# The sum over states in a Mamba scan: identity matmuls in VectorE's layout in place of accumulated transposes, a copy and transposes back

## What is computed

```python
def step(h, e):                      # h: (batch, 512 channels, 16 states)
    da, dbu, c = e
    h = da * h + dbu                 # the scan over time
    y = jnp.einsum('bdn,bn->bd', h, c)   # the sum over states
    return (h, y)
_, ys = jax.lax.scan(step, h0, elems)
y = jnp.moveaxis(ys, 0, 1) + u * D
y = y * jax.nn.silu(z)
out = jnp.einsum('bld,ed->ble', y, W_out)
```

## Time and profile before

| what | value |
|---|---|
| median of 3 runs | 1965.84 us (1965.61 to 1968.22) |
| span of the profiled execution | 1972.5 us, 16625 instructions |
| PE busy | 1592.9 us (81%) |
| DVE busy | 1595.6 us (81%) |
| ACT busy | 1005.4 us (51%) |
| POOL busy | 842.5 us (43%) |
| mean granted TensorE clock | 0.869 |

### The profile page before, as it was taken

One profiled execution on the slowest core, in us unless ns is written; L12 is line 12 of the kernel. 1 busy time (PEld: TensorE's weight loads), 2 busy tenths in 40 slices (PEclk: granted clock), 3 DMA queues, 4 the chain that ended last, 5 costly groups with the idle time before them and its releaser, 6 DMA issues. The chain is left out here.

```text
span 1972.5 us, 16625 instructions
## 1 busy us (share of the span) xinstructions
PE 1592.9 (81%) x5776; PEld 842.8 (43%) x5776; DVE 1595.6 (81%) x1686; ACT 1005.4 (51%) x1609; POOL 842.5 (43%) x443
## 2 busy tenths in 40 slices
PE   6767877798888789887888779987888879976954
PEld 2445334443455245543455235453445334452423
DVE  4895879957997989978998889979899789973264
ACT  4542755356563656446563655636553655633511
POOL 0764365515553265515554265614555155520000
PEclk9767788787899789997899889997899879987977
DMA  4000000000000000000000000000000000000000
GB/s 151 1 0 11 12 0 0 11 13 0 1 0 18 6 11 1 11 12 0 11 0 11 12 11 0 0 23 0 11 0 11 12 0 11 0 11 11 1 11 11
DMA packets 18057, 20.51 MB, mean 10 GB/s; under 512 B 1360, under 2 KB 16976, under 8 KB 18016
## 3 DMA queue, kind: packets, MB, share of 16 engines
q1 hardware_dynamic: 18016, 19.98, 3.1%
HBM read 15.79 MB, written 4.19 MB: 10 GB/s over the span
## 5 line engine op out<-in xcount | busy, mean ns | idle before, releaser
L393 POOL TENSOR_TENSOR reg_a<-reg_a,cb 128x1024 f32<-128x1024 f32 x256 | 603.7, 2359 | 495.9 <-DVE reg_a L1099 495.9
L1099 DVE TENSOR_TENSOR_SCAN reg_a<-reg_a,pb 128x1024 f32<-128x1024 f32 x256 | 584.2, 2282 | 22.3 <-ACT reg_a L858 12.5
L1089 DVE TENSOR_TENSOR pb<-pb,dtu 128x1024 f32<-128x1024 f32 x256 | 309.8, 1210 | 73.8 <-PE pb L591 69.3
L858 ACT ACTIVATE reg_a<-dt,neg_a 128x511 f32<-128x511 f32 x512 | 336.9, 710 | 46.7 <-DVE reg_a L1099 46.5
L612 PE MATMUL py<-ident,reg_a 128*128 128x128 f32 x2048 | 311.3, 303 | 21.8 <-POOL reg_a L393 21.8
L612 PEld LDWEIGHTS py<-ident,reg_a 128*128 128x128 f32 x2048 | 278.7, 158 | 76.1 <-POOL reg_a L393 25.3
L591 PE MATMUL pb<-bcs,sel 96*128 96x512 bf16 x512 | 179.9, 440 | 122.5 <-DVE reg_a L1099 118.4
L493 PE MATMUL px<-hT,whh 128*128 128x512 f32 x384 | 202.4, 653 | 0.0
L591 PEld LDWEIGHTS pb<-bcs,sel 96*128 96x128 bf16 x512 | 38.7, 103 | 276.8 <-DVE reg_a L1099 169.1
L760 ACT ACTIVATE xs<-px,half_b 128x512 f32<-128x512 f32 x96 | 66.0, 688 | 144.2 <-PE px L497 143.8
L570 PE MATMUL pc<-x2T,w_fc 128*128 128x512 f32 x224 | 109.9, 614 | 24.2 <-DVE reg_y L1113 11.7
(11 more groups left out here) (183 smaller groups left out, 2432.0 us busy)
## 6 DMA issues: line engine op xcount, KB each, us to landing
xin<-x_in SPq DMA_DIRECT2D x9, 512.0 KB, 3.5
xs<-x_in SPq DMA_DIRECT2D x8, 512.0 KB, 3.6
x_out<-reg_m SPq DMA_DIRECT2D x8, 512.0 KB, 3.0
w_in<-w_inT_in SPq DMA_DIRECT2D x1, 1024.0 KB, 6.9
w_fc<-w_fcT_in SPq DMA_DIRECT2D x1, 1024.0 KB, 10.9
w_pr<-w_prT_in SPq DMA_DIRECT2D x1, 1024.0 KB, 13.1
xs<-wihT_in SPq DMA_DIRECT2D x1, 768.0 KB, 8.8
whh<-whhT_in SPq DMA_DIRECT2D x1, 768.0 KB, 8.8
```

Source lines behind the costliest of these rows:

```text
L393: pool.tensor_tensor(h[:, g % HR], h[:, g % HR], cb[:, 2 * q:2 * q + 2], ALU.mult).then_inc(s["hc_done"], 1)
L858: ins = act.activation(d_a[:, g % 2, j, 1:], dt[:, c, 1:], ACT.Exp, scale=neg_a[:, c * NS + n + j:c * NS + n + j + 1])
L1089: dve.tensor_tensor(pb[:, b:b + 2, :], pb[:, b:b + 2, :], dtu[:, c:c + 1, :].to_broadcast([P, 2, L]), ALU.mult).then_inc(s["mul_done"], 1)
L1099: dve.tensor_tensor_scan(h2[:, g % HR], d_a2[:, g % 2], pb[:, b:b + 2, :].rearrange("p a t -> p (a t)"), 0.0, ALU.mult, ALU.add).then_inc( ...
```

## The change

`hsum` keeps the layout: the identity is stationary and h streams, 512 columns at a time, one plain float32 matmul for each of the two states, accumulated over the chunk in `py`. `y_back`, ACT's copy at line 877 and the `back` waits of the feed-forward units go. DVE's line 1113 reads `py` itself after the last `hsum` of its chunk, and the first `hsum` of the next chunk waits for line 1113 (`ypost_done`).

```diff
-                        if chunk_end(g) is not None:
-                            y_back(chunk_end(g), reads_before_slot(g) if ffn else 0)
                         if LAG <= g < GROUPS + LAG:
                             hsum(g - LAG)
...
                 c, q = g // PAIRS, g % PAIRS
                 pe.wait_ge(s["hc_done"], g + 1)
                 if q == 0 and c:
-                    pe.wait_ge(s["yt_ready"], c)
+                    pe.wait_ge(s["ypost_done"], c)
                 for j in range(2):
-                    for i2 in range(TT):
-                        cols_ = slice(i2 * P, (i2 + 1) * P)
-                        mm = pe.matmul(py[:, cols_], h[:, g % HR, j, cols_], ident[:], is_transpose=True,
-                                       start=(q == 0 and j == 0 and i2 == 0), stop=(q == PAIRS - 1 and j == 1), skip_group_check=True)
+                    mm = pe.matmul(py[:], ident[:], h[:, g % HR, j, :], start=(q == 0 and j == 0), stop=(q == PAIRS - 1 and j == 1))
                 mm.then_inc(s["hsum_done"], 1)
-
-            def y_back(c, reads):
-
-                if reads:
-                    pe.wait_ge(s["unit_read"], reads)
-                pe.wait_ge(s["yt_ready"], c + 1)
-                for i2 in range(TT):
-                    mm = pe.transpose(pc[:, i2 * P:(i2 + 1) * P], yv[:, c, i2 * P:(i2 + 1) * P], ident[:])
-                mm.then_inc(s["yback_full"], 1)
...
                 if reads > 0:
                     pe.wait_ge(s["unit_read"], reads)
-                if back:
-                    pe.wait_ge(s["ypost_done"], back)
...
-                        if g > LAG and (g - LAG) % PAIRS == PAIRS - 1:
-                            c = (g - LAG) // PAIRS
-                            act.wait_ge(s["hsum_done"], PAIRS * (c + 1))
-                            act.wait_ge(s["dt_ready"], DT)
-                            act.activation(yv[:, c], py[:], ACT.Copy).then_inc(s["yt_ready"], 1)
...
                             c = chunk_end(g)
-                            dve.wait_ge(s["yback_full"], c + 1)
-                            dve.scalar_tensor_tensor(yv[:, c], u2[:, c], half_d[:, c:c + 1], pc[:], ALU.mult, ALU.add).then_inc(s["ypost_done"], 1)
+                            dve.wait_ge(s["hsum_done"], PAIRS * (c + 1))
+                            dve.wait_ge(s["dt_ready"], DT)
+                            dve.scalar_tensor_tensor(yv[:, c], u2[:, c], half_d[:, c:c + 1], py[:], ALU.mult, ALU.add).then_inc(s["ypost_done"], 1)
```

More of the change, by code:

```diff
@@ L56 @@
 next_stat next_aggr next_ve next_rs next_norm next_full xnT_ready u_full pre_full upad_zero uacc_ready conv_step uth_ready u_ready
-z_full zth_ready sz_ready bc_split dtin_ready sp_abs sp_exp sp_ln dt_ready dtu_ready da_zero yt_ready yback_full
+z_full zth_ready sz_ready bc_split dtin_ready sp_abs sp_exp sp_ln dt_ready dtu_ready da_zero
 cb_full cb_ready bcb_full da_ready mul_done scan_done hc_done hsum_done ypost_done yz_done
@@ L269, in unit_bank @@
             return py[:] if not mamba and reads_before(half, name, j) % 2 else pc[:]
[L271 to L278, removed]
         def take(position, slot_step, mamba, slots, ffn, spikes):
@@ L285, in take @@
                     if kind in ("up", "down"):
-                        slot_step(*step, back=chunks_back(position) if mamba else 0, spikes=spikes, mamba=mamba)
+                        slot_step(*step, spikes=spikes, mamba=mamba)
                     else:
@@ L350, in _, with slot_step @@
             meet(pool, 1)
-            def slot_step(step, k=0, j=0, back=0, ffn=False, spikes=False, mamba=False):
+            def slot_step(step, k=0, j=0, ffn=False, spikes=False, mamba=False):
                 if (step, k) == ("ctx", 0):
@@ L508, in slot_step @@
                 elif step == "up":
-                    ffn_up(k, j, back, mamba)
+                    ffn_up(k, j, mamba)
                 elif step == "down":
-                    ffn_down(k, j, back, mamba)
+                    ffn_down(k, j, mamba)
                 elif step == "final":
@@ L554, in out_proj, with unit_start @@
                     mm.then_inc(s["op_half"], 1)
-            def unit_start(half, name, j, back, mamba):
+            def unit_start(half, name, j, mamba):
                 reads = reads_before(half, name, j) if mamba else reads_before(half, name, j) - 1
@@ L562, in unit_start, with ffn_up @@
                     pe.wait_ge(s["unit_read"], reads)
-                if back:
-                    pe.wait_ge(s["ypost_done"], back)
-            def ffn_up(half, j, back, mamba):
-                unit_start(half, "up", j, back, mamba)
+            def ffn_up(half, j, mamba):
+                unit_start(half, "up", j, mamba)
                 f = half * UPS + j
@@ L571, in ffn_up, with ffn_down @@
                 mm.then_inc(s["f_full"], 1)
-            def ffn_down(half, i2, back, mamba):
-                unit_start(half, "down", i2, back, mamba)
+            def ffn_down(half, i2, mamba):
+                unit_start(half, "down", i2, mamba)
                 pe.wait_ge(s["f_sq"], UPS * (half + 1))
```

## The result

The changed kernel takes 2139.55 us (median of 4 runs, 2137.63 to 2140.34), beside 1967.03 us for the kernel before on the same occasions: a ratio of 1.0874, interval 1.086 to 1.0889, slower by 172 us. The forecast was slower, 2105 us, with a range of 2060 to 2150.

What follows compares the result with a forecast made beforehand. DVE paces the loop, but in several stretches waits for a gapless PE. Six full iterations losing 119 us, iteration 1 losing 15 and iteration 0 losing 5.4 made +139 on 1965.8: 2105 us, range 2060 to 2150.

Steps and rivals of the forecast that it cites:

- The ledger: Slot-by-slot lateness of PE and DVE against the old timeline; a full iteration loses 19.8 us, the whole 139 us.
- first stretch, slots 4 to 8: Full iteration, up to line 502: longer sums make PE late, and all of it reaches DVE at line 993, +3.5 us.
- slot 34: End of the loop: copy and transposes back drop out, but DVE arrived late by its own queue, so nothing is gained.
- Slot 10, the new wait: Group 8's sum waits for line 1113; the filler behind it is 1.6 us later, and scan 11 loses 0.4 us.
- Slot 18: Group 16's sum waits for line 1113; PE is 10.1 us late, DVE not more than 7.6, covered by its filler.
- Slot 26: Group 24's sum waits for line 1113, with no DVE filler to cover it: DVE goes to 12.2 us late, PE 13.7.
- three uncovered sums of iteration 0: Iteration 0, without filler: sums behind line 1113 are uncovered three times, 3 x 1.8 = 5.4 us.
- first rival: The clock pays part back: plain matmuls instead of transposes raise PE's clock, 20 us gained in all, 2085 us; chance 0.22.
- All of it lands: Whole kernel: the full price, 206 us, plus 14 us of uncovered sums at line 1113, gives 2185 us; chance 0.06.
- Slack: PE's slack takes most; only line 993's two waits and their stretches carry it, +60 us, 2025 us; chance 0.08.
- faster case: A float32 identity matmul goes as one instruction of 0.43 us, so the sum is no longer than before: 1955 us; chance 0.03.

Runs made afterwards that it cites:

- early line 1113: The changed kernel with line 1113 moved on DVE ahead of the scan of its slot, matmul price kept: 2035.22 us, ratio 1.0334.
- doubled transposes: The kernel before with every transpose of the sum made twice, 16 instructions a group, no new wait: 2069.33 us, ratio 1.052.
- half sum with the early line 1113: The changed kernel with one of two identity matmuls a group left out and line 1113 ahead of its slot's scan: 1953.89 us, ratio 0.9938.
- kernel kept warm: The changed kernel with unused broadcast matmuls filling idle PE ahead of the first sum of a chunk, at ten places: 2120.62 us, ratio 1.0784.
- filler put first: The changed kernel with the sum of slots 10, 18 and 26 issued behind the slot's filler instead of ahead: 2083.86 us, ratio 1.0593.
- the wait and the short sum: Two kernels: the kernel before plus the wait for line 1113, 2025.79 us; the changed kernel with one identity matmul a group left out, 2025.19 us.
- bf16 sum: The changed kernel with POOL's product and the identity in bf16, and line 1113 ahead of its slot's scan: 1962.83 us, ratio 0.9981.
- extra broadcasts: The bf16 sum with the early line 1113, and every broadcast of B to its pair of banks made twice: 1975.94 us, ratio 1.0057.

## Why the prediction was right, and where its sum was off

Direction, range and the price of a group were right. That the total came within 35 us of the result is in part luck: of the 139 us forecast some 96 were price and some 43 the wait's steps, and measured in the changed structure they are 67 and 104 us. The one error took off nearly half of the other.

**The price of a group was right.** 1.72 us by the chain, 1024 instructions, against the earlier trace rows of line 493. The Trainium skill's factor of four between the two forms ("TensorE: Matmul & The Clock Gate", Terms) is not what these shapes show: 1024 columns take 1.72 us as plain matmuls and 0.88 as transposes, a factor of two, and the measurement decides.

**What of the price lands on the path was about right.** The ledger without its steps at slots 10, 18 and 26 gives about 13.5 us for a full iteration and 96 for the whole. The early line 1113, which has hardly any wait, shows 11.8 to 13.4 us (its 32 scans take 178.1 us in iteration 3 and 179.4 in iterations 5 and 7, against 166.1, 166.1 and 166.0), and the doubled transposes cost 101 us. The first stretch, slots 4 to 8, was forecast at 3.5 us; in the full iterations the scan of slot 9 comes 3.2 to 3.4 us later after than before. In the new structure the price is smaller, 67 to 81 us, since iteration 1 lost 1.6 us where I took 15 with its waits, iteration 2 8.7, and the half sum with the early line 1113 is 12 us below the kernel before, a gain that I had put at nothing. It gains in the stretches between the loops of scans (from the last scan of iteration 1 to the first of iteration 2, 52.6 us against 58.7). How much of that is the shorter chain of slot 34, forecast as no gain, was not taken apart.

**The term that was mis-sized is the new wait**, in the steps "Slot 10, the new wait", "Slot 18", "Slot 26", and the three uncovered sums of iteration 0. It was put at 1.6 + 2.5 + 2.2 us of PE's lateness in a full iteration, the growth of these sums themselves included, and 1.8 us each in iteration 0, some 43 us. It measured 104 us (the changed kernel less the one with line 1113 early). The mechanism was named, but costed as one sum at 1.72 us behind line 1113. Two things were left out. PE stands idle ahead of it, 65.0 us over 24 times, and at most places comes out of that at 1.2 GHz for part of the sum or all of it: 3.3 us on average, and 3.75 us at ten of the 24 (19 us came back at ten places by the kernel kept warm). And the waiting sum holds what is queued behind it, the feed-forward unit, the gates and, in iteration 0, the setup matmuls (56 us by the filler put first, part of it by less idle and a faster sum). In iteration 0 the loss was 16.3 us against 5.4. These two parts overlap with a third, the scan's own wait for the sum; how they add was not tried in one kernel.

**The rivals.** The clock did rise, from 0.869 to 0.908, as the first rival had it, and where PE does not idle for the wait to 0.929; but what the rise gave back no run isolates. Its reason does not hold: sixteen transposes a group were granted the same 0.929 as four instructions of plain matmuls. With the wait and the short sum it is 0.862 for transposes and 0.860 for plain matmuls. And with neither price nor wait, plain matmuls of the old length stay slow in iteration 0 as the transposes of the earlier trace rows do, 1.91 us (PE, half the sum and early):

```profile
108.24 1.91 PE L598 MATMUL py<-reg_a,ident 128*128 128x512 f32 x2
```

So the form of the sum did not change the granted clock; it went with how much PE has to do for a group. The Trainium skill says in the same page, PE-mode transpose, that transposes do not count as activity for the clock; here they did: doubling them raised it from 0.869 to 0.929, and the measurement decides. "All of it lands" (2185 us) was 45 us off, the forecast 35; it put 206 us on the price and 14 on the uncovered sums at line 1113, where 67 and 104 were measured. Slack took little, and the faster case fell with the count of 1024.

**What the profile was to show.** The instructions, 1.72 us a group, the broadcast's wait over 120 us and an unchanged end (236.7 us from the last scan, before and after) came so; the gate's wait came to 97.6, just short of the 100 named; the waits for the sum in iteration 0 were to be about 2 us and were 2.8, 4.0 and 3.9 us. The full iterations were to be 20 us longer, and their loops of scans are 25 to 27 us longer (iteration 2, which has the feed-forward for the first time, 22).

## What to carry to other kernels

When a change moves a hand-over from one engine's early instruction to another's late one, cost the receiving queue: the idle ahead of the waiting instruction, the clock it comes out with, and everything behind it. Here one semaphore wait, executed 24 times, cost 58 us even with the old matmuls, and moving the releasing instruction ahead of one scan and one product recovered 104 us. A layout change that saves a copy on an engine with slack and four transposes a chunk on PE is paid in longer passes of PE, which has little slack: two float32 matmuls of 512 columns took PE 1.72 us where the eight transposes that they replace took 0.88.

## What the hardware showed unexpectedly

Transposes and plain float32 matmuls of the same length (1.91 and 1.88 us a group) brought the same mean granted clock, 0.929. It went with how much PE does in the other runs too: 0.836 with the bf16 sum, 0.860 to 0.876 with a sum of 0.86 or 0.88 us in either form. The same idle of 2.06 us ahead of a sum left one at 1.96 us and another at 3.75 us. A rise of it from 0.836 to 0.869 by extra broadcasts went with 13 us more time.
